# GpSimd takes the subtraction of the softmax's maximum from VectorE in a masked attention

## The reference

```python
q = decoder_output @ wq_w + wq_b
k = encoder_output @ wk_w + wk_b
v = encoder_output @ wv_w + wv_b
...
score = jnp.einsum('bhqd,bhkd->bhqk', q, k) / jnp.sqrt(jnp.asarray(KEY_SIZE, dtype=jnp.float32))
score = score * mask
score = jnp.where(score == 0, jnp.float32(NEG_INF), score)
alignment = jax.nn.softmax(score, axis=-1)
context = jnp.einsum('bhqk,bhkd->bhqd', alignment, v)
...
x = _layernorm(x + _L1_xattn_ref(x, ctx_1024, mask_Bx1xSxS2_ff1, ...), axis=-1)
```

## Time and profile before

| | |
|---|---|
| median of 3 runs | 6432.54 us (6427.48 to 6441.0) |
| the profiled execution's span, first to last instruction | 6405.1 us |
| the profiled execution's own time | not given apart from the three runs; median less span is 27.4 us |
| mean granted TensorE clock | 0.912 |
| busy over the span | TensorE 5117.0, VectorE 4948.7, ScalarE 3333.2, GpSimd 3224.5 us |
| x1: first and last start of L825 | 4674.3 and 5113.6 us |

### The profile page before, as it was taken

One profiled execution on the slowest core, in us unless ns is written; L12 is line 12 of the kernel. 1 busy time (PEld: TensorE's weight loads), 2 busy tenths in 40 slices (PEclk: granted clock), 3 DMA queues, 4 the chain that ended last, 5 costly groups with the idle time before them and its releaser, 6 DMA issues. The chain is left out here.

```text
span 6405.1 us, 177571 instructions
## 1 busy us (share of the span) xinstructions
PE 5117.0 (80%) x62372; PEld 3049.9 (48%) x62372; DVE 4948.7 (77%) x10291; ACT 3333.2 (52%) x4888; POOL 3224.5 (50%) x3167
## 2 busy tenths in 40 slices
PE   6999999999999985887858758999866658777880
PEld 3444344444444333665655526676645446666440
DVE  5999999999999974997973355777589928888334
ACT  4666666666666652555722203444456527777440
POOL 4444454444445222665616564555433329888443
PEclk9999999999999996998979977999978869999995
DMA  1211111111111122211125530000011022222443
GB/s 48 50 46 47 51 44 50 43 51 44 50 48 44 49 66 64 58 46 40 42 58 137 129 112 12 18 17 17 10 39 32 24 58 73 73 73 71 131 131 106
DMA packets 620501, 368.28 MB, mean 57 GB/s; under 512 B 67337, under 2 KB 601292, under 8 KB 619852
## 3 DMA queue, kind: packets, MB, share of 16 engines
q1 hardware_dynamic: 598652, 333.12, 18.7%
q0 software_dynamic: 11648, 21.26, 1.7%
q10 hardware_dynamic: 9552, 5.58, 0.3%
HBM read 204.83 MB, written 66.85 MB: 42 GB/s over the span
## 5 line engine op out<-in xcount | busy, mean ns | idle before, releaser
L1401 ACT ACTIVATE mb_dA<-ps,mb_a_neg 128x1024 f32<-128x1024 f32 x1008 | 1122.9, 1114 | 811.7 <-PE ps L1159 797.2
L1838 DVE TENSOR_TENSOR mb_m<-mb_dA,ps 128x352 f32<-128x352 f32 x2016 | 956.3, 518 | 0.0
L1847 DVE TENSOR_TENSOR ps<-mb_m,ps 128x352 f32<-128x352 f32 x1984 | 949.0, 525 | 0.0
L1142 PE MATMUL ps<-mb_m,mb_ident 128*32 128x320 f32 x7936 | 741.5, 446 | 8.3 <-DVE mb_m L1831 1.4
L1191 PE MATMUL ps<-mb_m,mb_cz 128*32 128x256 f32 x8064 | 623.0, 381 | 34.9 <-issue 19.7
L1831 DVE TENSOR_TENSOR mb_m<-mb_dA,ps 128x320 f32<-128x320 f32 x1008 | 488.3, 484 | 98.0 <-PE ps L1142 80.4
L1174 PE MATMUL ps<-mb_ur,mb_bl 64*128 64x256 bf16 x4032 | 388.7, 271 | 53.7 <-DVE mb_m L1838 50.7
L1159 PE MATMUL ps<-mb_ur,mb_sel 64*128 64x256 bf16 x4032 | 396.6, 275 | 22.1 <-DMA mb_ur<-mb_pc 13.0
L1191 PEld LDWEIGHTS ps<-mb_m,mb_cz 128*32 128x32 f32 x8064 | 255.3, 110 | 327.9 <-issue 52.9
L678 POOL TENSOR_TENSOR x_p<-x_p,x_rec 128x2048 f32<-128x2048 f32 x64 | 231.7, 3620 | 212.3 <-DVE x_rec L839 212.3
L1697 POOL TENSOR_TENSOR mb_ys<-mb_ys,mb_cbu 128x256 f32<-128x256 f32 x64 | 46.8, 731 | 536.3 <-ACT mb_ys L1498 535.3
(11 more groups left out here) (507 smaller groups left out, 13291.5 us busy)
## 6 DMA issues: line engine op xcount, KB each, us to landing
mb_ur<-mb_pc SPq DMA_DIRECT2D x768, 64.0 KB
mb_bl<-mb_pc SPq DMA_DIRECT2D x576, 64.0 KB
ef_w<-in_ef_w SPq DMA_DIRECT2D x35, 514.5 KB
mx_w<-in_mx_w SPq DMA_DIRECT2D x39, 384.0 KB
moe_made<-mx_y SPq DMA_DIRECT2D x39, 256.0 KB, 2.4
ea_wqk<-in_ea_wqk SPq DMA_DIRECT2D x70, 129.0 KB
ea_wvo<-in_ea_wvo SPq DMA_DIRECT2D x70, 128.5 KB, 2.1
ea_x<-hidden SPq DMA_DIRECT2D x280, 32.0 KB, 2.0
```

The lines of the kernel that those rows point to most:

```text
L1142: mm = nc.tensor.matmul(out[c:c + 32], weights[:, c:c + 32], moving, start=start, stop=stop, skip_group_check=not grouped)
L1401: nc.scalar.activation(dA[:, t % RING].rearrange("p (g n) -> p g n", g=2), ps[:, DT:DT + 2, :], ACT.Exp, scale=a_neg[:, 0:1]).then_inc(dA_ ...
L1838: nc.vector.tensor_tensor(m[:, t % RING, cols], dA[:, t % RING, cols], state(u, t - 1, cols), ALU.mult).then_inc(md_ready.sem, 1)
L1847: nc.vector.tensor_tensor(h, m[:, t % RING, cols], h, ALU.add).then_inc(hd_ready.sem, 1)
```

## The change

In x1 only, four things:

- VectorE no longer subtracts `top` (L829); GpSimd does, in a new function `subtract_top(j + 1)`, placed ahead of its normalise(j). VectorE gets a wait ahead of L825, for the subtraction of the quad before, since `top` is single.
- VectorE makes the minimum L825 right behind the mark operation L807, ahead of sums(j).
- GpSimd waits for s_masked(j+1), the end of L807, ahead of tail_scale(j-2) and add_bias(j+2).
- ScalarE's scale(j-2) goes from its place ahead of take_p(j-1, 1) to the end of the period, behind take_o(j-1).

```diff
@@ ScalarE, period
-                    if tail != "none" and live(j - 2):
+                    if tail != "none" and mask is None and live(j - 2):
                         scale(j - 2, two)
                     if live(j - 1):
                         take_p(j - 1, 1)
...
                         take_o(j - 1, past)
+                    if mask is not None and live(j - 2):
+                        scale(j - 2, two)
@@ GpSimd
+                def subtract_top(i, u):
+
+                    pool.wait_ge(top_ready.sem, top_ready.at(i))
+                    v = p[:, u].rearrange("p (c k) -> p c k", k=64)
+                    nc.gpsimd.tensor_tensor(v, v, top[:].rearrange("p (c a) -> p c a", a=1).to_broadcast([128, 32, 64]),
+                                            ALU.subtract).then_inc(shifted.sem, 1)
...
+                    if mask is not None and live(j + 1):
+
+                        pool.wait_ge(s_masked.sem, s_masked.at(j + 1))
                     if tail != "none" and live(j - 2):
                         tail_scale(j - 2)
...
                         add_bias(j + 2, two)
+                    if mask is not None and live(j + 1):
+                        subtract_top(j + 1, (u + 1) % 4)
                     if live(j):
                         normalise(j, u)
@@ VectorE, softmax_shift
                     if mask is not None:
+                        dve.wait_ge(shifted.sem, shifted.at(i - 1))
                         nc.vector.tensor_reduce(top[:], src, AX.X, ALU.min).then_inc(top_ready.sem, 1)
-                    elif not rope:
+                        return
+                    if not rope:
                         softmax_top(i)
@@ VectorE, period
+                    if mask is not None and live(j + 1):
+                        softmax_shift(j + 1, one)
                     if live(j):
                         sums(j, u)
...
-                    if live(j + 1):
+                    if mask is None and live(j + 1):
                         softmax_shift(j + 1, one)
```

## The result

The changed kernel takes 6405.3 us in the median (6397.81 to 6406.94, 4 runs) against 6433.55 for the kernel before in the same comparison: ratio 0.995, interval 0.9937 to 0.9962, 28 us less. Forecast were 6386 and 46 us less. It is faster, by 0.6 of what the sum gave, and 6405.3 lies 0.7 us inside the upper end of the forecast's range (6357 to 6406).

A forecast was written before the change was run, and what follows sets the result against it. VectorE's instruction stream was taken as the bound. With late mask loads, first three steps 31.7 plus 28 at 12.85 (359.8) give 391.5 against 439.3, 47.8 less; about 2 lost at the end leaves 46: 6386.5 us, range 6357 to 6406.

The forecast's parts named there:

- port's short step of 11.8: Port shared by VectorE and GpSimd: minimum, subtraction, normalisation, then the next mark give a least step of 11.8 us.
- small work: GpSimd's L690 to L686, 2.1 us, now behind the mark: fits beside L825's 2.23 us, so costs nothing.
- reserve of the mask load: SyncE's mask load lands near 4871, wanted at 4877.8: 7 us to spare, forecast to be spent after the change.
- finish binds: VectorE's finish waits for scaled of the quad before; were the mask there, it would bind at 12.0 us a step.
- exclusive lock: Shared port: a GpSimd operation or a VectorE operation with two SBUF inputs holds it to its end.
- marks over 2.29 us in the first steps only: Sign on VectorE's L807: longer than 2.29 us only early; 3 us or more in steady steps would mean the port binds.
- VectorE's whole wait: VectorE idle some 2 us a step ahead of L803, the masking, released by the mask's DMA.
- The case that came true: Mask loads late on SyncE's queue: two steps 25.0 to 26.6 us, time 6386, 6377 to 6399; chance 0.60.
- a dearer subtraction of 4.7 us: Rival with GpSimd's subtraction at 4.7 us or lower TensorE clock: 13.4 us a step, 6405 us; chance 0.14.
- TensorE's turn: TensorE's turn after the normalisation: 1.09 us, or 1.97 at the lower clock; 1.25 taken as typical.
- ScalarE's part: ScalarE from first take of p to end of take_o: 6.52 and 6.15 us seen, 6.3 taken in the sum.
- alternation: L825-to-L825 steps come in pairs of about 25.7 us, alternating near 13.7 and 12.

The follow-up runs named there:

- mark from PSUM: Changed kernel with the mask load issued ahead of the store, plus the mark operation L807 comparing the raw PSUM score with zero: ratio 0.9925, 12.68 us a step.
- filled turn: Changed kernel plus 24 unread identity transposes on TensorE ahead of the first turn of p: ratio 0.992, 12.61 us a step.
- early mask load: Changed kernel with SyncE issuing quad k+4's mask load ahead of quad k's store: ratio 0.9917; with 16 transposes added, 0.9886.

## Why the prediction was right, and where its sum was off

Right, step by step. VectorE lost its subtraction, and GpSimd's costs 3.62 us (3.618 to 3.625). The port's short step of 11.8 is there at 11.74, with the mark held until 2.15 us after the normalisation. The new wait ahead of the minimum costs nothing, the small work hides beside it, the reciprocal keeps 0.35 under GpSimd's subtraction and the finish's copy 0.156 at most. The reserve of the mask load is spent and the load is waited for, behind scale and the store; taking it from there gives 21 us back, after which the finish binds at 12.6 a step, where the text had 12.0. Each of the two masking instructions keeps its 1.2 us under GpSimd's work, and the mark from PSUM stops waiting there. Of what the prediction names of the Trainium skill ("SBUF — State Buffer", section "Who interferes with whom"), the exclusive lock is borne out by the mark of 3.29. For a copy it says only that it can take both ports, when its operands meet conditions; the one-element copy of 0.15 is no test of wider ones, and no run here has one.

Not right in all of its signs. The text expected marks over 2.29 us in the first steps only, and gave 3 us or more in the steady steps as a sign that it was wrong and the port the bound. From the twelfth step on all short steps have 3.29 to 3.37. So the port does bind each second step; it does not set the time, since the mark from PSUM takes that standing away and the mean stays. The text also put VectorE's whole wait, 2 us a step, ahead of the masking; its size is right, but more of it (32.2 against 23.6 us) stands ahead of the finish.

The range was met with luck in it. The case that came true was given 6377 to 6399, and its two steps of 26.6 are the upper end of that; the time lies beyond it. The range reaches to 6406 for the sake of another case, a dearer subtraction of 4.7 us, which did not come: it took 3.62.

Off was the size, 46 us against 28, and in one term above all. The sum took 1.25 us for TensorE's turn and 11.3 from the normalisation's end to the mask's landing; measured are 1.97 and 12.2. ScalarE's part, 6.3 in the sum, is 6.48. Two steps are 26.6 instead of 25.7, 28 steps 372.6 us instead of 359.8: 12.8 of the difference. I had read the mix of both clock levels in a kernel where TensorE stood 1.8 and 2.4 us ahead of that turn and kept it for one where it stands 5.8 to 6.2 in the long steps from the twelfth on. The filled turn shows that the clock is the cause: with it up, two steps fall to 25.2. That is 1.4 us, more than the 0.9 that the sum was short of, because the sum already held a part of the lower clock's price: at the upper one the turn takes 1.09, not 1.25, and ScalarE's part 5.7, not 6.3. The alternation is sharper than forecast, 14.8 and 11.7 instead of 13.7 and 12; with the turn filled it is nearly gone (the last twenty steps are 11.8 to 13.3). The rest is small. The first three steps took 32.8 where I had 31.7, and from the last minimum to the next attention stage it is 130.6 instead of 126.0, 4.6 more where I had 2. Together 12.8 + 1.1 + 2.6 = 16.5, and 46 less 16.5 is 29.5, beside 29.3 in the traces.

So the parts of the change weigh thus: with scale in its new place, the subtraction on GpSimd and the early minimum gain only together (0.995 with both, 0.9991 and 1.0015 with one), while for the early minimum with the mask load in time that is open; the wait for the mark is worth nothing; scale's new place costs 13 us by the ratios, 18 by the traces. What the tail's 2.6 us more consist of was not looked into.

## What to carry to other kernels

When a full engine is relieved, work out the chain that spans two steps, through every queue that issues in order: here a load that had 7 us to spare was queued behind a store, and the store behind the operation that the change moved back. A faster step can make another engine wait longer in a lump, and here TensorE's turn cost 1.97 us after 5.9 us of standing and 1.09 after 1.4; a chain that is now critical should be summed with the durations of such steps, not with the mean of the full kernel. Of the orders tried on the two engines that share the port, the shortest step was the one in which GpSimd's two long operations follow each other without a gap and the mark, which must wait for them, comes last (11.7 us, against 12.1 with the normalisation first and 14.2 with the minimum behind the sums). And undo each part of a change with the others' side effects out of the way: a part can look worthless only because another one has made a load late.

## What the runs showed of the hardware that I had not expected

Useless work sped the kernel up: 24 transposes a step, 2.84 us of TensorE's time, took 19 us off the changed kernel and raised its granted clock from 0.87 to 0.99 over 300 us; 16 of them did the same beside the early mask load, 0.90 to 0.98 and 20 us. As the port came free, the VectorE operation that had stood for 1.2 us got it, and not the 2-column GpSimd operation behind the normalisation, which took 2.24 us instead of 0.20. And unchanged gather stages took 30 us more in some executions than in others (starts of mx_tk 3383.4 to 3589.0 and 3380.8 to 3616.2), as much as the whole change is worth; it went by the chip, all eight traces of two chips short and all three of the third long.
